# MoE combine weight as its square root ahead of the squaring, spread over partitions by DMA instead of by a matmul, and the low-part difference on GpSimd

## The reference

```python
def relu2(x):
    return jnp.square(jax.nn.relu(x))
tidx, tw = _route(xf, router_w, correction_bias)       # 8 of 64 experts, weights >= 0, sum 2.5
combine = jnp.zeros((T, E)).at[jnp.arange(T)[:, None], tidx].add(tw)      # T=2048, E=64
def body(acc, ew):
    wu, wd, c = ew                                     # wu 128x64, wd 64x128, c: one weight per token
    return (acc + c[:, None] * (relu2(xf @ wu) @ wd), None)
routed, _ = jax.lax.scan(body, zeros, (up_w, down_w, combine.T))
shared = relu2(xf @ shared_up_w) @ shared_down_w
```

## Time and profile before

| | us |
|---|---|
| median of the runs | 1312.22 |
| lowest run | 1310.79 |
| span of the profiled execution | 1317.5 |
| MoE stage, first up matmul to last down matmul, in the profiled execution | 233.0 to 453.3 |

### The profile page before, as it was taken

The page is one execution under the profiler, slowest core; times in us unless marked ns, Lnnn a source line. Parts: engine busy times, 40 slices in busy tenths (PEclk is TensorE's granted clock), DMA queues, the critical chain, the costliest instruction groups (busy, mean ns, idle before and its releaser), DMA issues.

```text
span 1317.5 us, 17710 instructions
## 1 busy us (share of the span) xinstructions
PE 1166.7 (89%) x6249; PEld 680.9 (52%) x6249; DVE 1046.4 (79%) x2018; ACT 776.6 (59%) x1151; POOL 43.9 (3%) x45
## 2 busy tenths in 40 slices
PE   3888647999999855779999999999998799999998
PEld 2333333666666512345444443443332688888886
DVE  4699998788888883879899889888851688888885
ACT  1635414899999710135555656566676566666664
POOL 0000020000000040140000000000000000000000
PEclk9898767899999956589999999999999699999999
DMA  5000000000000214551000000000000121111001
GB/s 161 0 0 1 0 24 17 16 17 16 18 14 1 78 35 79 72 78 16 2 2 2 1 1 2 1 1 1 1 1 1 45 102 56 56 56 56 0 1 33
DMA packets 38169, 35.02 MB, mean 27 GB/s; under 512 B 15162, under 2 KB 33530, under 8 KB 36810
## 3 DMA queue, kind: packets, MB, share of 16 engines
q1 hardware_dynamic: 36082, 31.12, 9.0%
q0 software_dynamic: 2016, 2.96, 1.7%
HBM read 30.85 MB, written 3.08 MB: 26 GB/s over the span
## 4 chain that ended last, share of the span: by engine, by line
PE 61%; DVE 26%; ACT 6%; issue 3%; DMA 3%; SPq 1%; DVEq 0%; ACTq 0%
PE ps L822 10%; PE ps L823 10%; PE ps L824 10%; PE ps L983 9%; DVE arena_a L1766 7%; PE ps L927 7%; PE ps L971 6%; DVE arena_b L1472 3%; DVE mv L1377 2%; PE ps L839 1%; ACT arena_b L1222 1%; DMA arena_a<-q_parts 1%; PE ps L693 1%; DMA arena_a<-arena_a 1%; DVE xn L1384 1%
## 5 line engine op out<-in xcount | busy, mean ns | idle before, releaser
L1766 DVE TENSOR_REDUCE arena_a<-ps 128x1 f32<-128x512 f32 (+3 forms) x560 | 344.4, 668 | 73.2 <-PE ps L931 46.3
L1289 ACT ACTIVATE arena_b<-ps 128x1024 f32<-128x1024 f32 (+3 forms) x320 | 274.0, 894 | 191.8 <-PE ps L971 169.6
L822 PE MATMUL ps<-parts 128*128 128x512 f32 x640 | 273.2, 427 | 7.1 <-DVE parts L1688 4.2
L823 PE MATMUL ps<-parts 128*128 128x512 f32 x640 | 251.5, 393 | 0.0
L824 PE MATMUL ps<-parts 128*128 128x512 f32 x640 | 251.2, 392 | 0.0
L927 PE MATMUL ps<-arena_b,arena_a 128*128 128x512 bf16 (+3 forms) x576 | 190.4, 354 | 6.3 <-DVE arena_a L1766 4.9
L971 PE MATMUL ps<-arena_a,arena_b 128*128 128x512 bf16 (+3 forms) x576 | 163.2, 348 | 0.7 <-ACT arena_b L1289 0.3
L983 PE MATMUL ps<-arena_b 128*32 128x512 f32 (+3 forms) x1280 | 151.1, 544 | 2.5 <-DVE arena_b L1754 2.2
L822 PEld LDWEIGHTS ps<-parts 128*128 128x128 f32 x640 | 122.0, 191 | 36.8 <-DVE parts L1688 9.7
L824 PEld LDWEIGHTS ps<-parts 128*128 128x128 f32 x640 | 121.0, 189 | 26.4
L823 PEld LDWEIGHTS ps<-parts 128*128 128x128 f32 x640 | 121.4, 190 | 22.4
(11 more groups left out here) (274 smaller groups left out, 1445.3 us busy)
## 6 DMA issues: line engine op xcount, KB each, us to landing
arena_b<-expert_weights SPq DMA_DIRECT2D x7, 1024.0 KB, 6.7
arena_a<-q_parts SPq DMA_DIRECT2D x18, 128.0 KB
arena_a<-q_parts POOLq DMA_DIRECT2D x18, 128.0 KB, 5.9
wslot<-in_L_ffn_up_w SPq DMA_DIRECT2D x8, 256.0 KB, 3.1
wslot<-in_L_ffn_down_w SPq DMA_DIRECT2D x8, 256.0 KB, 3.3
wslot<-in_L_ffn_w_gate SPq DMA_DIRECT2D x8, 256.0 KB, 2.9
wslot<-in_L_ffn_w_up SPq DMA_DIRECT2D x8, 256.0 KB, 3.4
wslot<-in_L_ffn_w_down SPq DMA_DIRECT2D x8, 256.0 KB, 3.8
```

What stands on the lines that cost most here:

```text
L822: mm(bank, w(0), x(0), start=start, stop=False)
L823: mm(bank, w(0), x(1), start=False, stop=False)
L1289: a(probs[:, s % 2, 2 * pair:2 * pair + 2, off:CW], ps[:, 2 + 2 * pair:4 + 2 * pair, off:CW], ACT.Exp, scale=scale).then_inc(p2_exp, 1)
L1766: v.tensor_reduce(mx[:, n % 2, i:i + fit, t % TPC, u], b[:, 0:fit * w].rearrange("p (h k) -> p h k", k=w), AX_X, ALU.max)\
```

## The change

1. **Algebra.** c·relu(u)² = (√c·relu(u))². DVE now makes `prod0` = max(u, 0)·√c in one instruction from PSUM (L1673 of the changed kernel), ACT squares it twice, once to fp32 and once to the fp32r high part (L1245, L1246), and GpSimd makes the low part (L673).
2. **Root.** After the combine weights, ACT takes the square root of 128 x 1024 values, DVE refines it with one Newton step (max, reciprocal, two more instructions, L1646 to L1649), PE transposes 16 fp32 tiles, ACT copies them out (`scT`).
3. **Spreading.** SP stores the roots to a DRAM tensor `root_weights` [64, 2048] (4 DMAs), waits for them, and then loads for each pair two rows, each repeated over 64 partitions, into one of 4 SBUF buffers `cbw` (`load_cb`, 1024 KB, 32 times). DVE waits for a pair's load (`ld_cb`) at its first unit; SP issues the load of pair p once DVE has finished pair p-4.
4. **PE.** The bf16 matmul and its `sel` matrix go away. `look0` now has 4 banks instead of 2.

The core of the diff:

```diff
+            def load_cb(buf, pair):
+                sp.dma_start(cbw[:, buf, :], sc_dram[bass.ds(2 * pair, 2), :].unsqueeze(1).broadcast_to([2, I0, T]))\
+                  .then_inc(ld_cb[buf], 16)
+            for pair in range(NCBUF):
+                load_cb(pair, pair)
+            for pair in range(NCBUF, 2 * GP):
+                sp.wait_ge(moe_prod, NC * (pair - NCBUF + 1))
+                load_cb(pair % NCBUF, pair)
             with sp.Fori(1, N_IT0) as it:
                 for slot in range(2):
                     sp.wait_ge(w0_lo, it * 4 + (2 * slot - 2))
                     load0(slot, it * 2 + slot)
+                    for k in range(GP):
+                        pair = slot * GP + k
+                        sp.wait_ge(moe_prod, it * MU + NC * (pair - NCBUF + 1))
+                        load_cb(pair % NCBUF, it * (2 * GP) + pair)
...
+            def low_unit(n0, k):
+                pool.wait_ge(moe_sq, n0 + (k + 1))
+                pool.wait_ge(moe_hi, n0 + (k + 1))
+                nc.gpsimd.tensor_tensor(hid0[:, k % NBUF, 1, :], sq0[:, k % NBUF, :],
+                                        hid0[:, k % NBUF, 0, :].bitcast(F32), ALU.subtract).then_inc(moe_lo, 1)
...
-                w = sel[0:NCB, bass.ds(base + pair % GP, 1), :].rearrange("p a f -> p (a f)")
-                mm(ps[:, 2 + k % 2, :], w, combT[0:NCB, slot, chunk(c)], start=True, stop=True).then_inc(moe_cb, 1)
...
-                a(hid0[:, k % NBUF, 0, :], prod0[:, k % NBUF, :], ACT.Copy).then_inc(moe_hi, 1)
+                a(sq0[:, k % NBUF, :], prod0[:, k % NBUF, :], ACT.Square).then_inc(moe_sq, 1)
+                a(hid0[:, k % NBUF, 0, :], prod0[:, k % NBUF, :], ACT.Square).then_inc(moe_hi, 1)
...
+            dve.wait_ge(rt0_ready, 1)
+            chain(v.tensor_scalar(msk, b2, 1e-18, None, ALU.max))
+            chain(v.reciprocal(sfc, msk))
+            chain(v.scalar_tensor_tensor(sfc, b1, 0.5, sfc, ALU.mult, ALU.mult))
+            v.scalar_tensor_tensor(b1, b2, 0.5, sfc, ALU.mult, ALU.add).then_inc(root_ready, 1)
...
+                pair, c = k // NC, k % NC
+                if c == 0:
+                    dve.wait_ge(ld_cb[pair % NCBUF], it * (16 * 2 * GP // NCBUF) + 16 * (pair // NCBUF + 1))
+                dve.wait_ge(moe_up, n0 + (k + 1))
+                v.scalar_tensor_tensor(prod0[:, k % NBUF, :], ps[:, k % 4, :], 0.0, cbw[:, pair % NCBUF, chunk(c)],
+                                       ALU.max, ALU.mult).then_inc(moe_prod, 1)
```

More of the change, by code:

```diff
@@ L652, in _ @@
             pool.wait_ge(vzero, 2)
+            def low_unit(n0, k):
[3 more added lines that the diff above has]
+                                        hid0[:, k % NBUF, 0, :].bitcast(F32), ALU.subtract).then_inc(moe_lo, 1)
+            with pool.Fori(0, N_IT0) as it:
+                for k in range(MU):
+                    low_unit(it * MU, k)
             pool.wait_ge(x2_ready, NC)
@@ L824, in three, with look0 @@
                 return mm(bank, w(1), x(0), start=False, stop=stop)
-            def look0(base, k, n0, loads):
+            def look0(k, n0, loads):
                 pair, c = k // NC, k % NC
@@ L831, in look0 @@
                     pe.wait_ge(w0_lo, loads)
-                if n0 is not None:
-                    pe.wait_ge(moe_relu, n0 + (k - 1))
-                three(ps[:, k % 2, :], lambda i: up0(slot, i, pair % GP), lambda i: hs0[:, i, chunk(c)],
+                if n0 is None:
+                    pe.wait_ge(comb_T, k + 1)
+                else:
+                    pe.wait_ge(moe_prod, n0 + (k - 3))
+                three(ps[:, k % 4, :], lambda i: up0(slot, i, pair % GP), lambda i: hs0[:, i, chunk(c)],
                       True, True).then_inc(moe_up, 1)
-                if n0 is not None:
-                    pe.wait_ge(moe_prod, n0 + (k - 1))
-                w = sel[0:NCB, bass.ds(base + pair % GP, 1), :].rearrange("p a f -> p (a f)")
-                mm(ps[:, 2 + k % 2, :], w, combT[0:NCB, slot, chunk(c)], start=True, stop=True).then_inc(moe_cb, 1)
             def sum0(n0, k, last_one):
@@ L849, in _ @@
             for k in range(LOOK):
-                look0(0, k, 0 if k >= 2 else None, 2)
-            with pe.Fori(0, N_IT0 - 1) as it:
+                look0(k, None, 2)
+            look0(LOOK, None, 2)
+            sum0(0, 0, False)
+            for k in range(1, MU):
+                if k + LOOK < MU:
+                    look0(k + LOOK, 0, 4)
+                else:
+                    look0(k + LOOK - MU, MU, 6)
+                sum0(0, k, False)
+            with pe.Fori(1, N_IT0 - 1) as it:
                 for k in range(MU):
                     if k + LOOK < MU:
-                        look0(it * GP, k + LOOK, it * MU, it * 4 + 4)
+                        look0(k + LOOK, it * MU, it * 4 + 4)
                     else:
-                        look0(it * GP + GP, k + LOOK - MU, it * MU + MU, it * 4 + 6)
+                        look0(k + LOOK - MU, it * MU + MU, it * 4 + 6)
                     sum0(it * MU, k, False)
```

132 lines of the change are left out of this document (33 added, 99 removed).

## The result

The changed kernel takes 1764.05 us (median of its runs, 1760.35 to 1766.49), the kernel before 1312.22 us beside it: ratio 1.344, 95% interval 1.338 to 1.351. It is slower by 452 us. A fourth run of the kernel before took 2832.59 us, where the other three took 1310.79 to 1313.79, and is left out. The profiled execution has a span of 1761.6 us. The prediction was 1771 us with a range of 1740 to 1820.

The account below looks back on a forecast made before the run. PE and ACT bound the old loop; two DMA engines the new. First load 242.7, plus 2.1, 32 x 20.2, weights 12 and 7.9 end it at 911.1, +457.8; with 1 for the clock, 1312.2 + 459 = 1771 us, range 1740 to 1820.

Parts of the forecast that it names:

- Two engines per load: Root loads in the MoE loop: each runs on 2 of the 16 DMA engines, 64 runs of 8 KB on each.
- The price of a load: Root loads: two engines give 52.0 GB/s, so 1.049 MB takes 20.2 us, at least 19.8.
- The way in: Before the loop: weights ready at 224.15, roots at 235.1, transposes and copy to 240.2, first root load issued at 242.7.
- The weights' loads: Six loads inside the loop, some 2 us each on every engine: 12 us more, with no gap for the two engines.
- The sum: Loop end: last root load lands at 903.2, 7.9 us follow, so 911.1 instead of 453.3, +457.8 us.
- PE's saving is hidden: MoE loop: one matmul of seven less would give back 37 us, but all of it is hidden.
- The fast rival: All 16 engines serve a root load, so the kernel takes 1292 us; chance 0.07.
- GpSimd: Its difference in each loop unit takes 0.43 to 1.29 us, under PE's 1.39, so the sum is unchanged.
- GpSimd is the bound: Rival for the loop: with fast loads and 2.0 us a unit on GpSimd, 1363 us; chance 0.03.
- Signs that I named: Changed profile: root loads 60 to 80 us to landing, DVE idle some 14 us a pair, PE's clock 0.50.

Follow-up runs that it names:

- experiment 1: Changed kernel with each root load reading one row for 128 partitions instead of two rows for 64 each: 1292.4 us.
- experiment 3: Changed kernel with the roots stored twice, so that a root load reads 4 rows 32 times each: 1456.4 us.
- experiment 5: Changed kernel with hidden unit f of expert e on partition 2f + e, the root load's 64 repeats outermost, weights following: 1297.9 us.
- experiment 4: Changed kernel with the loop's weights' loads issued from ACT's own queue, half a group earlier, instead of SP's queue: 1769.6 us.
- experiment 6: Kernel of experiment 5 with each root load as two one-row transfers, each onto every second partition: 1295.2 us.
- experiment 7: Kernel of experiment 5 with each unit's low-part difference on DVE instead of GpSimd, one unit behind the product: 1285.5 us.
- experiment 2: Changed kernel with each root load split in two transfers, one row to the lower and one to the upper 64 partitions: 1311.1 us.
- experiment 8: Kernel of experiment 7 plus a GpSimd difference in 120 of the 128 units that nobody needs: 1350.0 us.

## Why the prediction was right, step by step

- **Two engines per load.** Right, and it is the whole result. Shown by the trace (12.6%, two completion writes a load) and by experiments 1, 3 and 5, in which the outermost count moves a load from 19.76 to 9.89 to about 2.5 us; the last was the same with one row and with two. The step that carried it was the count of missing completion writes at the kernel's start.
- **The price of a load.** 20.2 us against 19.76, just under the lower bound of 19.8; over 31 loads that is 14 us, the largest miss of the sum.
- **The way in.** From the weights to the roots 10.9 us, as predicted (234.00 - 223.09). The weights were ready 1.1 us earlier, the transposes took 3.6 us for 4.4. The first root load was issued at 240.59 for 242.7. Issue to first product: 22.6 us for 22.3.
- **The weights' loads.** 12 us predicted. 891.29 - 263.20 = 628.1 us for 31 pairs, less 31 x 19.76, leaves 15.5, or 2.6 us for each of six. That there would be no gap in the two engines was right: the rate never falls, and experiment 4 shows it from the other side. The picture behind it was not: I had four loads queued at all times, but SP is held from the third load on, so fewer stand there.
- **The sum.** These together put the loop's end at about 900 us instead of 911.1. The span is 14 us under 1776, the time 7 us under 1771, mostly because the profiled execution of the kernel before was itself 5.3 us above the median of its runs. The largest miss is the 14 us of the price, and nothing of that size stands against it.
- **PE's saving is hidden.** Right. At 1.00 PE starts a matmul every 0.228 us in the fast kernels, 1.37 us a unit, but in the changed kernel it is idle for two thirds of the loop.
- **The fast rival** was given 1292 us and 0.07: experiments 1, 5 and 6 gave 1292.4, 1297.9 and 1295.2. Its time was right, its terms only in sum. The first product was 3 us earlier than I had it. The loop lost 10.4 us to the pace of PE (185.8 us from first to last product, against 128 x 1.37 = 175.4), where I had 5 for the weights' pieces and 2 for the clock. In experiment 7, without GpSimd, the loop lasts 176.9 us: 8.9 of the 10.4 are gone.
- **GpSimd.** Its difference takes 1.295 us, the upper bound (1.29). The estimate of 1.12 us, from the Trainium skill, GPSIMD Engine Reference, section 3.1, was too low. What I left out of the step is that it slows another engine: I compared 1.29 with PE's 1.39 and called it hidden. It is hidden in the changed kernel, where everything is; in a fast one it costs 12 us. The rival "GpSimd is the bound" named the pace of GpSimd itself, and that was never the case in these kernels.
- **Signs that I named.** The landing time of root loads isn't shown by the profile; instead SP is held. DVE waited 17.3 us a pair and not 14, since I took a pair's four products as spread out at PE's pace; they run back to back in 2.48 us. The granted clock was 0.62 as a mean of the stretch.

What stays open: why the six weights' loads cost 2.6 us each rather than 2.0, which port each DMA engine uses, and why experiment 4 is 5.6 us above the changed kernel by its one run.

## What to carry to other kernels

Write a DRAM-to-SBUF spread so that the outermost count of the source is a multiple of 16 (here 2 and 4 gave 2 and 4 engines, 64 and 128 gave all 16), and check in the DMA view that share and rate fit 16 engines: a share of 0.13 can be two engines at their limit. If two rows have to be spread, put the repeats outermost and let the rows alternate over the partitions. Before you move work to an idle GpSimd, ask which DVE instructions beside it read two SBUF tiles.

## What the runs showed that I had not expected

- **SP is held in issuing.** With two engines per load, eight root loads kept SP for 117.4 us, and in experiment 4 all 32 for some 594 of 608.9 us; in experiment 1 a load takes SP 0.34 us in the median. What stands behind them on SP's queue is late even where its semaphore has long come: the first load of up weights in the loop is issued at 358.39 us, though it waits only for the low parts made ahead of the loop.
- **64 neighbouring partitions are half as fast as 64 spread ones.** 213 GB/s against 438 GB/s, with 16 engines busy in both (experiments 2 and 6).
- **Work that nobody waits for costs 64 us** (experiment 8), by making a DVE instruction 1.166 us long instead of 0.686.
- **The longest wait on the chain was a symptom.** 240 us of waiting for the weights' load could be taken away whole, and the time went from 1764 to 1770 us.
